# Attention factors from one product and a transpose, and shifts spread over partitions by a product, in the preparation of a two-layer graph kernel

## What is computed

```python
# layer 0: graph attention with rank-one scores
x_l     = (x @ W + b).reshape(N, 8, 64)
alpha_l = einsum('nhc,hc->nh', x_l, att_l)
alpha_r = einsum('nhc,hc->nh', x_l, att_r)
scores  = alpha_l[:, None, :] * alpha_r[None, :, :]
att     = softmax(where(adj > 0, scores, -9e15), axis=1)
x       = layernorm(x + relu(einsum('ijh,jhc->ihc', att, x_l)))
# layer 1: dot-product attention; queries x, keys x2, values v
scores  = einsum('hnd,hmd->hnm', q * 64 ** -0.5, k)
x       = layernorm(x + softmax(where(adj > 0, scores, -9e15)) @ v)
```

## Time and profile before

| | us |
|---|---|
| median of three runs | 3744.48 (3743.8 to 3744.56) |
| the profiled execution | 3745.04 |
| its span in the profile | 3743.1 |
| preparation, first comparison to last copy of alpha_nat | 339.94 |
| PE busy in the span | 3551.1 (95%) |
| VectorE | 2909.1 (78%) |
| ScalarE | 2525.6 (67%) |
| GpSimd | 1569.5 (42%) |

### The profile page before, as it was taken

How to read it: one execution, slowest core, us unless ns; L and a number is a source line. 1 busy time by engine, 2 the same in 40 slices (tenths; PEclk the granted TensorE clock), 3 DMA queues, 4 the chain that set the end, 5 groups by cost and what they waited for, 6 DMA issues and landing times. The chain is left out here.

```text
span 3743.1 us, 58557 instructions
## 1 busy us (share of the span) xinstructions
PE 3551.1 (95%) x22661; PEld 1448.4 (39%) x22661; DVE 2909.1 (78%) x2948; ACT 2525.6 (67%) x2430; POOL 1569.5 (42%) x1157
## 2 busy tenths in 40 slices
PE   6888899999999999987699999999999999999987
PEld 4665222222222222225344444444444444444434
DVE  5555899999999999977577777777777777777768
ACT  3444899999999999963466666666666666666642
POOL 3333010010010101011267666767666677667661
PEclk9999899999999999995699999999999999999995
DMA  7887677677777776667699999999999999999987
GB/s 259 298 299 245 153 161 165 152 160 156 162 160 161 154 160 153 153 157 254 174 198 198 205 205 201 208 197 199 204 205 200 205 201 198 205 202 203 191 188 247
DMA packets 375357, 729.43 MB, mean 195 GB/s; under 512 B 31376, under 2 KB 219792, under 8 KB 358720
## 3 DMA queue, kind: packets, MB, share of 16 engines
q0 software_dynamic: 99504, 419.90, 57.7%
q1 hardware_dynamic: 241552, 272.26, 23.8%
q10 hardware_dynamic: 34048, 33.82, 2.7%
HBM read 263.54 MB, written 59.69 MB: 86 GB/s over the span
## 5 line engine op out<-in xcount | busy, mean ns | idle before, releaser
L1130 DVE TENSOR_TENSOR a_weights<-a_psS,maskT 128x1024 f32<-128x1024 f32 x1024 | 1205.5, 1219 | 463.5 <-ACT a_psS L1095 463.5
L1095 ACT ACTIVATE a_psS<-a_psS,a_shift 128x1024 f32<-128x1024 f32 x1024 | 1071.4, 1084 | 678.8 <-PE a_psS L1023 678.7
L538 DVE TENSOR_TENSOR g_weights<-g_weights,maskT 128x1024 f32<-128x1024 f32 x1024 | 1169.7, 1218 | 117.5 <-ACT g_weights L525 117.5
L525 ACT ACTIVATE g_weights<-al_bc,g_shift,g_xl 128x1024 f32<-128x1024 f32 x1024 | 1167.9, 1228 | 88.4 <-PE g_psD L563 88.4
L1023 PE MATMUL a_psS<-a_q,a_k 128*64 128x512 f16 x8192 | 971.6, 380 | 17.0 <-DMA a_k<-k_scratch 15.5
L1040 PE MATMUL a_psO<-a_weights,a_v 128*64 128x512 f32 x4096 | 961.2, 592 | 0.0
L554 PE MATMUL g_psO<-g_weights,g_xl 128*64 128x512 f32 x4096 | 924.1, 598 | 23.2 <-DVE g_weights L538 23.2
L1153 POOL TENSOR_TENSOR a_pool_total<-a_pool_total,a_weights 128x1024 f32<-128x1024 f32 x336 | 924.3, 2751 | 0.0
L1023 PEld LDWEIGHTS a_psS<-a_q,a_k 128*64 128x64 f16 x8192 | 463.4, 110 | 647.0 <-issue 300.4
L1161 POOL DMA_DIRECT2D a_dma_total<-a_weights x480 | 467.1, 973 | 399.6 <-DVE a_weights L1130 202.5
L554 PEld LDWEIGHTS g_psO<-g_weights,g_xl 128*64 128x64 f32 x4096 | 277.9, 137 | 660.5 <-issue 530.8
(11 more groups left out here) (121 smaller groups left out, 1451.0 us busy)
## 6 DMA issues: line engine op xcount, KB each, us to landing
a_dma_total<-a_weights POOLq DMA_DIRECT2D x512, 512.0 KB, 5.4
g_total<-g_weights POOLq DMA_DIRECT2D x128, 1024.0 KB, 7.7
adj_sb<-in_adj_dram SPq DMA_DIRECT2D x128, 512.0 KB, 5.9
g_xl<-xl_scratch SPq DMA_DIRECT2D x128, 260.0 KB, 6.7
a_k<-k_scratch SPq DMA_DIRECT2D x256, 128.0 KB, 5.4
a_v<-in_L_gnn_v_dram SPq DMA_DIRECT2D x128, 256.0 KB, 3.9
al_bc<-alpha_scratch SPq DMA_DIRECT2D x16, 1024.0 KB, 6.7
f_oT<-o_scratch SPq DMA_DIRECT2D x16, 1024.0 KB, 6.8
```

The lines of the kernel that those rows point to most:

```text
L525: nc.scalar.activation(w[:, u % RING, h, :], al_bc[:, g % 2, h, :], ACT.Exp, bias=shift_bc[:, g % 2, h:h + 1], scale=xl[:, slot, u % KB, 2 ...
L538: nc.vector.tensor_tensor(w[:, u % RING, h, :], w[:, u % RING, h, :], maskT[:, j, (g // PAIRS) * IC:(g // PAIRS + 1) * IC], ALU.mult).then ...
L1095: nc.scalar.activation(psS[n % RING][:], psS[n % RING][:], ACT.Exp, bias=shift_bc[:, g % 2, h:h + 1], scale=SCALE).then_inc(exped, 1)
L1130: nc.vector.tensor_tensor(w[:, u % NP, h, :], psS[n % RING][:].rearrange("p a c -> p (a c)"), maskT[:, j, (g // PAIRS) * IC:(g // PAIRS + ...
```

## The change

The eight-column product alpha_nat becomes a forty-column product `xT` by `wa` without the bias row. VectorE adds the bias part, which lies in the fifth block of `wa` in every partition, once into xl_sb and once into a new tile al_sb (128x128, cleared at the start, of which 40 columns are used). PE transposes al_sb between the turns of quarters 2 and 3, and VectorE copies the transpose to alphaT. The products of L329, L331 and L332 are gone. The order of VectorE and PE gets two new semaphores.

In the tail each shift is multiplied with the identity's first eight rows into `spread` (8x8), and one product with rows of ones puts all sixteen shifts into every partition; they stay in the kept tile `shift_bc`, from which both attention stages read their bias. The stores and loads of the shifts are gone. GpSimd's stores of the column sums and of the head mask wait for the column sums alone.

```diff
@@ prepare, GpSimd
-            pool.wait_ge(tail_dve, 3)
+            pool.wait_ge(tail_dve, 1)
             pool.dma_start(col_dram[0], colsum[:]).then_inc(heads_stored, 16)
             pool.dma_start(head_dram, headmask[:]).then_inc(heads_stored, 16)
-            for layer in range(2):
-                pool.dma_start(shift_dram[layer].rearrange("(h o) -> h o", o=1), shift[:, layer:layer + 1]
-                               ).then_inc(shift_stored, 16)
-            pool.wait_ge(shift_stored, 32)
-            pool.dma_start(bounds[:], shift_dram[:, :].rearrange("(o a) h -> o a h", o=1)).then_inc(shift_stored, 16)
@@ prepare, PE
                     for c in range(4):
-                        nc.tensor.matmul(alpha_nat, xT[:, k, c, :], wa[:, c, 32:40], start=(c == 0), stop=False)
-                    nc.tensor.matmul(alpha_nat, onesF[0:1, :], wa[0:1, 4, 32:40], start=False, stop=True)
-                    for c in range(4):
-                        nc.tensor.matmul(alpha_T, wa[:, c, :], xT[:, k, c, :], start=(c == 0), stop=False)
-                    nc.tensor.matmul(alpha_T, wa[0:1, 4, :], onesF[0:1, :], start=False,
-                                     stop=True).then_inc(alpha_ready[k], 1)
+                        last = nc.tensor.matmul(alpha_nat, xT[:, k, c, :], wa[:, c, :], start=(c == 0), stop=(c == 3))
+                    last.then_inc(alpha_ready[k], 1)
                     turn_mask(t, 2)
+                    pe.wait_ge(alpha_biased, t + 1)
+                    nc.tensor.transpose(psA[:, P:2 * P], al_sb[:], identF[:]).then_inc(alpha_turned, 1)
                     turn_mask(t, 3)
...
+            pe.wait_ge(shift_spread, 2)
+            nc.tensor.matmul(psA[:, 0:2 * H], onesF[0:H, :], spread[:].rearrange("p a h -> p (a h)"), start=True,
+                             stop=True).then_inc(tail_pe, 1)
@@ prepare, VectorE
+            nc.vector.memset(al_sb[:], 0.0)
...
                     dve.wait_ge(alpha_ready[k], m + 1)
-                    nc.vector.tensor_copy(xl_sb[:, k, :, 2 * C:XW],
-                                          alpha_nat.rearrange("p (a h) -> p a h", h=2)).then_inc(xl_done[k], 1)
+                    nc.vector.tensor_tensor(xl_sb[:, k, :, 2 * C:XW], alpha_nat[:, 32:40].rearrange("p (a h) -> p a h", h=2),
+                                            wa[:, 4, 32:40].rearrange("p (a h) -> p a h", h=2),
+                                            ALU.add).then_inc(xl_done[k], 1)
+                    nc.vector.tensor_tensor(al_sb[:, 0:40], alpha_nat, wa[:, 4, :], ALU.add).then_inc(alpha_biased, 1)
                     if s == 0:
                         dve.wait_ge(al_stored, r * 32)
+                    dve.wait_ge(alpha_turned, t + 1)
                     nc.vector.tensor_copy(alphaT[:, s * P:(s + 1) * P], alpha_T).then_inc(alpha_done, 1)
...
-            nc.vector.tensor_scalar(shift[:, 0:1], ext_r[:, 1:2], -1.0, None, ALU.mult).then_inc(tail_dve, 1)
+            then(nc.vector.tensor_scalar(shift[:, 0:1], ext_r[:, 1:2], -1.0, None, ALU.mult))
+            nc.vector.tensor_scalar(spread[:, 0, :], identF[0:H, 0:H], shift[:, 0:1], None, ALU.mult).then_inc(shift_spread, 1)
...
-            nc.vector.tensor_scalar(shift[:, 1:2], reach[:], -1.0, None, ALU.mult).then_inc(tail_dve, 1)
-            dve.wait_ge(shift_stored, 48)
-            then(nc.vector.tensor_reduce(least[:], bounds[:], AX.X, ALU.min))
+            then(nc.vector.tensor_scalar(shift[:, 1:2], reach[:], -1.0, None, ALU.mult))
+            nc.vector.tensor_scalar(spread[:, 1, :], identF[0:H, 0:H], shift[:, 1:2], None, ALU.mult).then_inc(shift_spread, 1)
+            dve.wait_ge(tail_pe, 3)
+            then(nc.vector.tensor_copy(shift_bc[:].rearrange("p a h -> p (a h)"), psA[:, 0:2 * H]))
+            then(nc.vector.tensor_reduce(least[:], shift_bc[0:1, :, :], AX.X, ALU.min))
@@ attend_gat (attend_dot has the same, with its 80 becoming 64 and shift_bc[:, 1, ...])
-                sp.dma_start(shift_bc[:, par, :], shift_dram[0, pair * 2:pair * 2 + 2].partition_broadcast(P)
-                             ).then_inc(const_loaded[par], 16)
-                    act.wait_ge(const_loaded[g % 2], 32 * (g // 2 + 1))
+                    act.wait_ge(const_loaded[g % 2], 16 * (g // 2 + 1))
-                                         bias=shift_bc[:, g % 2, h:h + 1],
+                                         bias=shift_bc[:, 0, g % PAIRS * 2 + h:g % PAIRS * 2 + h + 1],
```

More of the change, by code:

```diff
@@ L66, in gat_resnorm_kernel @@
         wide = sb("wide", [1, 2], I32)
-        prepare(nc, keep, x, adj, W, b, att_l, att_r, x2, xl_dram, al_dram, k_dram, shift_dram,
-                col_dram, head_dram, maskT, identF, onesF, wide)
+        shift_bc = sb("shift_bc", [P, 2, H], F32)
+        prepare(nc, keep, x, adj, W, b, att_l, att_r, x2, xl_dram, al_dram, k_dram,
+                col_dram, head_dram, maskT, identF, onesF, shift_bc, wide)
         sems = semaphores_of_either(nc, keep, 0)
@@ L74, in gat_resnorm_kernel @@
         with nc.Else():
[L75 removed]
+            attend_gat(nc, sems(), xl_dram, al_dram, shift_bc, v, o_dram, d_dram, vsum_dram, maskT, onesF)
         finish_layer(nc, keep, 0, x, o_dram, d_dram, x1_dram, q_dram, col_dram, vsum_dram, head_dram, identF, onesF)
@@ L80, in gat_resnorm_kernel @@
         with nc.Else():
-            attend_dot(nc, sems(), v, q_dram, k_dram, shift_dram, o_dram, d_dram, maskT, onesF)
+            attend_dot(nc, sems(), v, q_dram, k_dram, shift_bc, o_dram, d_dram, maskT, onesF)
         finish_layer(nc, keep, 1, x1_dram, o_dram, d_dram, out, None, col_dram, None, None, identF, onesF)
@@ L98, in semaphores_of_either, with prepare @@
     return way
-def prepare(nc, keep, x, adj, W, b, att_l, att_r, x2, xl_dram, al_dram, k_dram, shift_dram,
-            col_dram, head_dram, maskT, identF, onesF, wide):
+def prepare(nc, keep, x, adj, W, b, att_l, att_r, x2, xl_dram, al_dram, k_dram,
+            col_dram, head_dram, maskT, identF, onesF, shift_bc, wide):
     ctx = ExitStack()
@@ L135, in prepare @@
         xl_sum = sb("xl_sum", [P, F], F32)
+        al_sb = sb("al_sb", [P, P], F32)
         alphaT = sb("alphaT", [40, KB * P], F32)
@@ L142, in prepare @@
         reach = sb("reach", [H, 1], F32)
-        bounds = sb("bounds", [1, 2, H], F32)
+        spread = sb("spread", [H, 2, H], F32)
         least = sb("least", [1, 2], F32)
@@ L150, in prepare @@
         psM = [ps(f"psM{i}", [P, JB, P], BF16) for i in range(4)]
-        alpha_nat = psA[:, 0:H]
+        alpha_nat = psA[:, 0:40]
         alpha_T = psA[0:40, P:2 * P]
@@ L175, in prepare @@
         xl_done = [sem(f"xl_done{i}") for i in range(2)]
+        alpha_biased = sem("alpha_biased")
+        alpha_turned = sem("alpha_turned")
         alpha_done = sem("alpha_done")
@@ L183, in prepare @@
         ext_step = sem("ext_step")
-        shift_stored = sem("shift_stored")
+        shift_spread = sem("shift_spread")
         heads_stored = sem("heads_stored")
@@ L432, in attend_gat @@
         al_bc = sb("al_bc", [P, 2, 2, IC], F32)
-        shift_bc = sb("g_shift", [P, 2, 2], F32)
         xl = sb("g_xl", [P, XS, KB, XW], F32)
@@ L896, in _, with attend_dot @@
                 nc.vector.tensor_tensor(next_sum[:], psO[0][0:H, :], headmask[:], ALU.mult).then_inc(tail, 1)
-def attend_dot(nc, sem, v, q_dram, k_dram, shift_dram, o_dram, d_dram, maskT, onesF):
+def attend_dot(nc, sem, v, q_dram, k_dram, shift_bc, o_dram, d_dram, maskT, onesF):
     ctx = ExitStack()
@@ L912, in attend_dot @@
         q_sb = sb("q", [P, 2, 2, 2, IC], F16)
-        shift_bc = sb("shift", [P, 2, 2], F32)
         k_sb = sb("k", [P, 2, 2, KB * P], F16)
@@ L1011, in scores @@
                 if j == 0:
-                    pe.wait_ge(q_loaded[par], 80 * (g // 2 + 1))
+                    pe.wait_ge(q_loaded[par], 64 * (g // 2 + 1))
                 if u % KB == 0:
@@ L1090, in _ @@
                 if j == 0:
-                    act.wait_ge(q_loaded[g % 2], 80 * (g // 2 + 1))
+                    act.wait_ge(q_loaded[g % 2], 64 * (g // 2 + 1))
                 for h in range(2):
@@ L1095, in _ @@
                     nc.scalar.activation(psS[n % RING][:], psS[n % RING][:], ACT.Exp,
-                                         bias=shift_bc[:, g % 2, h:h + 1], scale=SCALE).then_inc(exped, 1)
+                                         bias=shift_bc[:, 1, g % PAIRS * 2 + h:g % PAIRS * 2 + h + 1], scale=SCALE
+                                         ).then_inc(exped, 1)
                 if g > 0 and j == 1:
```

6 lines of the change are left out of this document (1 added, 5 removed).

## The result

The changed kernel takes 3723.4 us (median of six runs, 3722.33 to 3724.65) beside 3742.98 us (3739.49 to 3744.56): a ratio of 0.9948, 95% interval 0.9936 to 0.9961. It is faster by some 20 us, where 41 were forecast. The profiled execution has a span of 3721.7 us.

The account below looks back on a forecast made before the run. PE is at work through 89% of the preparation loop and VectorE waits for it. Loop -34.9, tail -4.2, attention starts -1.6 and -0.6 sum to -41.3 us, giving 3703 us, range 3684 to 3727.

Parts of the forecast that it names:

- Round ends: Loop, end of each four-tile round: later alphaT mostly hidden while the comparison waits; +0.8 us in all, at worst 5.6.
- the first projections: Loop, first projection of each round: no change in time forecast, 0 us.
- the factor products: Loop, each tile: first factor product to first VectorE add falls from 2.64 to 1.0 us; -52.5 us over 32 tiles.
- the wait of PE for the biased factors: Loop, PE's new wait on alpha_biased: at most 0.4 us a tile, taken at nothing; up to 13 us without cover.
- the order in which GpSimd comes first: Loop, two tiles of four: GpSimd's sum precedes the comparison, so A to projection is 4.24 us, not 3.19; +16.8 us.
- the tail: After the last tile: shifts no longer go through DRAM; -4.2 us, between -3 and -5.2.
- The head mask's store: Tail, GpSimd: issued at about 367.8, waiting only for column sums; lands at about 370.2 and ends the stage.
- sq would hold a comparison issued ahead of it: Loop: sq, 2.12 us after A, holds the second comparison; by the skill's rule the sum would be 16.8 us lower.
- rival 1: Loop: second comparison goes first, projection 3.19 us after A in 16 tiles, no 16.8 us loss; 3686; chance 0.15.
- the starts of the attention stages: Shift loads leave SP's queue: -1.6 us at the graph attention's start, -0.6 us at the second attention's.
- the first g_shift load: Graph attention's first group: it holds SP's queue 1.50 us ahead of g_xl; its removal gives -1.6 us, 0 to -2.1.
- Rival 2: Loop: PE's clock falls in each tile, the other 24 projections lose 0.8 us each, 19 us back; 3722; chance 0.15.

Follow-up runs that it names:

- e_no_sum: The changed kernel without GpSimd's running sum of the projections (column sums are zero): 3708.56 us, ratio 0.9911.
- e_alpha_first: The changed kernel with the two alphaT stores of a round issued ahead of the two keys' stores: 3704.03 us, ratio 0.9893.
- e_before_alpha_first: The kernel before with the two alphaT stores issued ahead of the keys' stores: 3734.53 us, ratio 0.9978.
- e_factors_only: The kernel before with only the changed factor products, transpose and VectorE adds; bounds, shift loads and old tile places as before: 3722.61 us, ratio 0.9949.
- e_same_places: The changed kernel with shift_bc padded by 448 bytes and al_sb last, so old tiles keep their remainder by 512: 3720.03 us, ratio 0.9937.

## Why the prediction was wrong

**The step that failed** is this one, in its words: "Round ends. The comparison there waits for the extremes, and these wait for sq ... I take 0.1 us in 8 rounds: +0.8 us (at worst 5.6)." It costed the round end on VectorE's way alone. VectorE did as said (comparisons 3.86 us after A in both). But ScalarE's way, four stores, a table load and xT, ends last there, and it grew by 1.07 us. The forecast names the stores at the round end and gives them no term. In the kernel before the omission did not show, since the two ways ended nearly together: xT is done at 197.03 + 0.60 = 197.63, 0.36 us ahead of the projection. In the kernel after it is done at 187.00, and the projection starts 0.13 us behind it. Round ends cost 6.5 us, and the first projections, which the forecast left at their clock of before, 9.8: 16.3 us instead of 0.8. With the stores out of the way the step is right again: with them ahead of the keys' stores in both kernels, the loop from first projection to last A goes from 330.34 to 298.03 us, -32.3 against a forecast of -34.9. The round ends then differ by 6.08 - 6.00 = 0.08 us, near the 0.1 of the forecast, and the first projections by 0.01.

**Right:** the factor products (2.64 to 1.03, forecast 1.0; -51.5 of -52.5), the wait of PE for the biased factors (nothing, as taken), the order in which GpSimd comes first (+17.5 of +16.8, and the projection 4.24 to 4.33 us after A of 4.24), and the tail (-3.6 of -4.2). The head mask's store is issued 349.06 - 343.78 = 5.28 us after the last A (forecast 367.8 - 362.50 = 5.3), lands 7.8 us after it (7.7) and ends the stage, as the forecast has it; the 0.6 that is missing is 2.1 us from this landing to the next load, against 1.53 from wide. (The 2 us that the forecast takes for the reload are 2.25 by the times that it names; they are 2.06 to VectorE's first step on it, at 374.11.) That sq would hold a comparison issued ahead of it is confirmed by e_no_sum. The Trainium skill's rule in "SBUF — State Buffer", section "Who interferes with whom", that the one issued first has the shared ports, does not agree with these rows, as far as the trace's starts on GpSimd go; by it rival 1 would have come true.

**Off by a size:** the starts of the attention stages. Of -1.6 us for the first g_shift load, 0.7 came: g_xl is issued 354.07 - 353.63 = 0.44 us after al_bc instead of 377.98 - 375.99 = 1.99, but its two issues now take 2.09 us instead of 0.99, directly behind the 1 MB of al_bc. That looks like the stores of alphaT behind the keys' stores; it was not tried by itself. Of -0.6 us in the second attention nothing came. Its first load and PE's first product, in the kernel before and then after:

```profile
1825.42 3.78 SPq L964 DMA_DIRECT2D a_q<-q_scratch  x4
...
1834.74 4.40 PE L1023 MATMUL a_psS<-a_q,a_k 128*64 128x512 f16 x24 [15.54 <-DMA a_k<-k_scratch]
```
```profile
1803.86 3.52 SPq L966 DMA_DIRECT2D a_q<-q_scratch  x4
...
1814.82 4.13 PE L1023 MATMUL a_psS<-a_q,a_k 128*64 128x512 f16 x24 [17.16 <-DMA a_k<-k_scratch]
```

The keys are issued earlier without a_shift, but PE gets them 10.96 us after the first load instead of 9.32; over the kernels run here this start takes 9.3 to 12.0 us. In all, from the first load of the graph attention to the end of the program the kernel after takes 3721.7 - 353.63 = 3368.1 us against 3743.1 - 375.99 = 3367.1: +1.0 where -2.2 was forecast. This stretch varies from 3365 to 3371 us over the kernels run here, also where nothing in it differs, and what sets it is open; it takes back 4.9 us of what e_alpha_first gains on e_before_alpha_first.

**Rival 2** named the right kind of loss, the clock, but in the wrong place: the clock is low in the first tile of each round, for longer than before, and not in the other 24, whose projections take 3.49 us. That its 3722 us lies beside the measured 3723.4 is chance: it has 24 tiles lose 0.8 us each, and what was lost is 16.3 us at the ends and in the first tiles of the rounds.

**Open:** why, with the keys' tiles at their old places, the second store of alphaT takes 1.10 us as soon as the factor part is changed (e_factors_only, e_same_places), though ScalarE's own program is the same. It needs the keys' stores in front, since ahead of them it takes 0.31 (e_alpha_first). That these land later is not enough: in the rounds of e_factors_only they do (4.7 and 6.1 us after issue instead of 2.9 and 4.3), but in its last round they land after 2.9 and 4.3 us, as in the kernel before, and the second store takes 1.10 us there too, against 0.35.

**A version that beats both:** the change with one store of 40 rows, 3699.7 us behind the keys' stores and 3698.56 ahead of them: 44 us under the kernel before.

## What to carry to other kernels

Where an edit shortens one engine's way through a loop, go through every engine's program at the place where the loop turns, the queues that issue DMAs first: a small store behind a large one can hold its engine three times as long as alone, so issue the small ones ahead, or as one. A wait of one microsecond at such a place may cost more by PE's clock afterwards than by itself (here 16 us and 7). And before a new tile is put in, see what it pushes off a multiple of 256 bytes: move the pad alone to know its price.

## What was not expected of the hardware

Sixty-four bytes that nothing reads made the kernel before 11 us slower (3753.83 against 3742.94), and 256 bytes left it as it was. The issue of one and the same store took 0.30 us with nothing of the keys ahead of it in its queue (0.61 at most, in the first round), and up to 1.15 us behind them. And 3.6 us of needless products at the start of each round, about as long as the first projection itself, gave 16 us back.
